# Decoder layer on one core: own order of each engine before the first scores, a transposed maximum, and another bank for eight turns

## The reference, cut to what matters

```python
x = x + attn(layernorm(x), wq, wk, wv, wo)       # 32 query heads, 8 key/value heads, rotary, causal softmax
x = x + einsum("emk,enk->emn",
               quant_1x128(layernorm(x)),        # scale per row and block of 128
               quant_128x128(ctx_2048))          # scale per block of 128 x 128
x = x + moe(layernorm(x), Wg, W1, W3, W2, sw1, sw3, sw2)
# quant_128x128: amax = max |w| over a block of 128 rows and 128 columns, w in fp8 of w * 448 / amax
```

## Time and profile before

| | |
|---|---|
| median of 3 runs | 1612.51 us (1610.12 to 1615.79) |
| the profiled execution's own time | 1612.85 us |
| its span | 1611.0 us |
| PE busy | 1465.1 us (91%) |
| DVE busy | 1213.7 us (75%) |
| POOL busy | 1020.4 us (63%) |
| ACT busy | 948.4 us (59%) |
| chain that ended last | PE 68%, DVE 14%, ACT 7%, issue 5% |

### The profile page before, as it was taken

The page is one execution under the profiler, slowest core; times in us unless marked ns, Lnnn a source line. Parts: engine busy times, 40 slices in busy tenths (PEclk is TensorE's granted clock), DMA queues, the critical chain, the costliest instruction groups (busy, mean ns, idle before and its releaser), DMA issues.

```text
span 1611.0 us, 26917 instructions
## 1 busy us (share of the span) xinstructions
PE 1465.1 (91%) x8616; PEld 1280.9 (80%) x8616; DVE 1213.7 (75%) x2951; ACT 948.4 (59%) x2384; POOL 1020.4 (63%) x1007
## 2 busy tenths in 40 slices
PE   5799999999798999999999998676989899899997
PEld 4588888887677888888888887565788888799996
DVE  6678888887777777878878787986767665587785
ACT  2477787776466678877878878523121213565662
POOL 1687887885776788888888888642303132354555
PEclk9899999999899999999999999897899999899998
DMA  5345444333132334334434433123010002577777
GB/s 188 98 126 165 135 134 134 109 87 100 49 102 50 88 85 118 98 90 115 113 81 109 120 81 89 33 88 91 27 27 27 8 27 84 176 240 221 227 217 239
DMA packets 106588, 177.04 MB, mean 110 GB/s; under 512 B 16662, under 2 KB 38422, under 8 KB 106448
## 3 DMA queue, kind: packets, MB, share of 16 engines
q1 hardware_dynamic: 103888, 167.07, 35.8%
q0 software_dynamic: 2560, 8.25, 1.6%
HBM read 97.28 MB, written 31.98 MB: 80 GB/s over the span
## 4 chain that ended last, share of the span: by engine, by line
PE 68%; DVE 14%; ACT 7%; issue 5%; DMA 2%; POOL 2%; SPq 1%; DVEq 0%; ACTq 0%; POOLq 0%
PE bank L417 15%; PE bank L419 14%; PE bank L418 14%; PE bank L459 6%; PE bank L435 4%; PE bank L474 4%; PE bank L475 4%; PE bank L436 4%; ACT P L762 3%; PE bank L409 2%; DVE P L1038 2%; DVE Opair L1073 1%; ACT xnx L784 1%; DVE work L987 1%; ACT Otmp L768 1%
## 5 line engine op out<-in xcount | busy, mean ns | idle before, releaser
L762 ACT ACTIVATE P<-P,mn 128x512 f32<-128x512 f32 (+3 forms) x512 | 285.0, 557 | 222.5 <-DVE mn L1038 218.9
L1444 POOL TENSOR_TENSOR P<-P,ri 128x128 f32<-128x128 f32 (+3 forms) x512 | 360.2, 735 | 30.2 <-DVE ri L1027 30.2
L1038 DVE CUSTOM_DVE_ANT_0 P<-bank,mask 128x512 f32<-128x512 f32 (+3 forms) x512 | 236.7, 481 | 117.6 <-PE bank L436 116.0
L1079 DVE TENSOR_TENSOR PTl<-bank,PTh 128x512 fp32r<-128x512 f32 (+1 forms) x384 | 229.6, 599 | 33.4 <-ACT PTh L774 30.8
L459 PE MATMUL bank<-ident,P 128*128 128x128 f32 x1280 | 204.7, 275 | 6.9 <-POOL P L1444 6.9
L435 PE MATMUL bank<-KT,QT 128*128 128x256 f32 (+2 forms) x512 | 190.7, 373 | 17.5 <-DVE mn L1038 17.3
L774 ACT ACTIVATE PTh<-bank 128x512 fp32r<-128x512 f32 (+1 forms) x384 | 197.4, 515 | 12.9 <-PE bank L459 10.0
L417 PE MATMUL bank<-XT,Wh 128*128 128x512 f32 x384 | 166.0, 432 | 11.1 <-DVE qcs L1051 6.2
L474 PE MATMUL bank<-PTh,VS 128*128 128x256 f32 (+2 forms) x512 | 163.6, 330 | 13.0 <-DVE PTl L1079 8.7
L436 PE MATMUL bank<-KT,QT 128*128 128x256 f32 (+2 forms) x512 | 167.7, 328 | 0.0
L459 PEld LDWEIGHTS bank<-ident,P 128*128 128x128 f32 x1280 | 151.8, 141 | 7.7 <-POOL P L1444 7.6
(11 more groups left out here) (194 smaller groups left out, 4237.8 us busy)
## 6 DMA issues: line engine op xcount, KB each, us to landing
RW<-in_wf SPq DMA_DIRECT2D x170, 256.0 KB, 3.1
QT<-qh SPq DMA_DIRECT2D x256, 64.0 KB, 2.0
QT<-ql SPq DMA_DIRECT2D x256, 64.0 KB, 2.0
Oraw<-in_wo SPq DMA_DIRECT2D x16, 512.0 KB, 5.3
KT<-KT SPq DMA_DIRECT2D x32, 256.0 KB, 3.0
xnx<-in_ctx SPq DMA_DIRECT2D x32, 256.0 KB, 3.4
Wraw<-in_wqkv SPq DMA_DIRECT2D x9, 768.0 KB, 5.3
saved<-Wh SPq DMA_DIRECT2D x7, 768.0 KB, 3.5
```

Source lines behind the costliest of these rows:

```text
L762: e.activation(pq, pq, ACT.Exp, bias=mn[:, z, qb:qb + 1], scale=-1.0, accum_out=rs[:, z, qb:qb + 1]).then_inc(a_exp, 1)
L1038: e.tensor_tensor_reduce(P[:, z, off[qb]:off[qb] + k], bank[n % 2][:, 0:k], mask[:, 512 - k:512], -0.125, BIG, ALU.add, ALU.min, mn[:, z, ...
L1079: e.tensor_tensor(pt_part(PTl, part), bank[2 + part][:, 0:128 * n].rearrange("p (m n) -> p m n", n=128), pt_part(PTh, part).bitcast(F32), ...
L1444: e.tensor_tensor(pq, pq, ri[:, z, qb:qb + 1].to_broadcast([128, n]), ALU.mult).then_inc(g_norm, 1)
```

## The change

Four things are changed; the arithmetic of the output stays.

1. The loop starts at h = 0. What was in h = -8 to -1 is written out ahead of it for each engine in an order of its own. ACT splits all three parts of the first weights ahead of its first copies. PE projects unit 0 in one piece, turns tiles 4 to 7 in banks 0 to 3, turns the values, and projects unit 1 in one piece. DVE takes the four rotations of unit 0 between the statistics of batch 1 and their inverse deviations. POOL makes `ql` of unit 0 ahead of the key's rotation; before it came behind. SP issues the keys' and queries' DMAs of unit 0 in one row.
2. DVE's statistics of batches 2 and 3 move into h = 0 to 3, two tiles in each, and their inverse deviations to h = 5.
3. Tiles 8 to 15 are turned in bank 2 in place of bank 5. `first_turn` waits for the readers of `turn_p(h - 2, 0)`, and the next `turn_p(..., 0)` waits for the readers of the turned tile.
4. The maximum over partitions is taken by a transpose on PE at h = 46 (128 x 64 into a free part of bank 4), a DVE reduction of 64 x 128, a DMA of the 64 numbers to DRAM at h = 48 and one that spreads them over 128 partitions at h = 49. `turn_p(45, 2)` waits for the reduction. `context_scales` moves from h = 49 to h = 51. POOL's call goes.

The core of the diff:

```diff
+AT_PEAK = 46
@@ wait_bank5
-            elif user == "first_turn":
-                need.wait_ge(v_x, h - 6)
-            elif h == 3:
-                wait_xt(need, 6)
             elif h < 8 or h - 8 >= NH - 11:
...
-            elif 52 <= h - 1 < 60:
-                wait_xt(need, h - 44)
@@ PE: turn_v
-                else:
-                    wait_xt(need, 5)
+                need.wait_ge(v_vl, u)
@@ PE
+            def turn_maxima():
+                need.wait_ge(v_cmax, NCTX)
+                need.wait_ge(a_pt, 3 * (AT_PEAK - 2))
+                need.wait_ge(v_pt, 3 * (AT_PEAK - 2))
+                e.transpose(bank[4][0:64, 256:384], wam[:, :, :].rearrange("p i c -> p (i c)"), ident[:, :]).then_inc(p_cmax, 1)
@@ PE: turn_p
+                if part == 0 and 51 <= h < 59:
+                    wait_xt(need, h - 42)
+                if part == 2 and h == AT_PEAK - 1:
+                    need.wait_ge(v_peak, 1)
@@ PE: ahead of the loop
-            for h in range(-8, NH + 7):
+            for part in range(3):
+                for c in range(4):
+                    project(0, part, c)
+            for t in range(TB, 2 * TB):
+                wait_xt(need, t - TB + 1)
+                first_turn(t, t - TB)
+            turn_v(0)
+            for part in range(3):
+                for c in range(4):
+                    project(1, part, c)
+            for h in range(NH + 7):
@@ PE: in the loop
+                if h == AT_PEAK:
+                    turn_maxima()
...
                 if 52 <= h < 60:
-                    wait_bank5(need, h, "first_turn")
-                    first_turn(h - 44, 5)
+                    need.wait_ge(a_pt, 3 * (h - 2) + 1)
+                    need.wait_ge(v_pt, 3 * (h - 2) + 1)
+                    first_turn(h - 44, 2)
@@ ACT: ahead of the loop
+            for part in range(3):
+                split_wq(0, part)
             for t in range(TB):
                 first_turn(t, t)
-                if t < 3:
-                    split_wq(0, t)
+            values_keys(0)
+            for t in range(TB, 2 * TB):
+                first_turn(t, t - TB)
+            query_hi(0)
+            value_hi(0)
+            key_hi(0)
+            split_wq(1, 0)
+            split_wq(1, 1)
@@ DVE
+            def context_peak():
+                need.wait_ge(p_cmax, 1)
+                e.tensor_reduce(wsc[0:64, 1, 0:1], bank[4][0:64, 256:384], AX.X, ALU.max).then_inc(v_peak, 1)
             def context_scales():
-                need.wait_ge(g_call, 1)
+                need.wait_ge(d_peak[1], 16)
@@ DVE: ahead of the loop, behind first_stats of tiles 4 to 7
+            for fn in range(2):
+                rotate(0, 0, fn)
+            for fn in range(2):
+                rotate(0, 1, fn)
             rstd_of(slice(TB, 2 * TB))
             for t in range(TB, 2 * TB):
                 first_norm(t)
+            key_cos(0)
+            for t in range(TB, 2 * TB):
+                first_turn(t, t - TB)
+            value_lo(0)
+            for fn in range(2):
+                rotate(1, 0, fn)
+            for fn in range(2):
+                rotate(1, 1, fn)
@@ DVE: in the loop
-                if h == 49:
+                if h == AT_PEAK + 5:
                     context_scales()
...
+                if h == AT_PEAK:
+                    context_peak()
...
-                elif h < 0:
-                    first_stats(2 * h + 16)
-                    first_stats(2 * h + 17)
-                if h == -1:
+                if h < 4:
+                    first_stats(2 * h + 8)
+                    first_stats(2 * h + 9)
+                if h == 5:
                     rstd_of(slice(2 * TB, 4 * TB))
@@ POOL: ahead of the loop
+            rotate(0)
+            query_lo(0)
+            rotate_key(0)
+            key_lo(0)
+            split_wq_lo(1, 0)
+            rotate(1)
@@ POOL: in the loop
-                if h == 45:
-                    need.wait_ge(v_cmax, NCTX)
-                    e.partition_all_reduce(wsc[:, 0, :], wam[:, :, :].rearrange("p i c -> p (i c)"), 128,
-                                           bass.bass_isa.ReduceOp.max).then_inc(g_call, 1)
@@ SP: ahead of the loop, behind load_wo(0)
+            load_wq(1)
+            turn_keys(0)
+            place_queries(0, 0)
+            place_queries(0, 1)
+            double_keys(0)
@@ SP: in the loop
+                if h == AT_PEAK + 2:
+                    need.wait_ge(v_peak, 1)
+                    e.dma_start(peak.unsqueeze(1), wsc[0:64, 1, 0:1]).then_inc(d_peak[0], 16)
+                if h == AT_PEAK + 3:
+                    need.wait_ge(d_peak[0], 16)
+                    e.dma_start(wsc[:, 0, :], peak.partition_broadcast(128)).then_inc(d_peak[1], 16)
```

More of the change, by code:

```diff
@@ L182, in decoder @@
         saved = nc.dram_tensor("saved", (NSAVE, 2, 128, 4, 384), F32).ap()
+        peak = nc.dram_tensor("peak", (4 * NCTX,), F32).ap()
         oe = nc.dram_tensor("oe", (NE * CAP, D), F32).ap()
@@ L214, in decoder @@
         v_bm, v_bq, g_badd, g_bq = sem("v_bm"), sem("v_bq"), sem("g_badd"), sem("g_bq")
+        p_cmax, v_peak, d_peak = sem("p_cmax"), sem("v_peak"), [sem("d_peak_out"), sem("d_peak_in")]
         v_cmax, v_cscale, v_q, v_turn, v_x2, v_xn3, v_lt, v_cum, v_place, v_idx, v_piece, v_hm, v_h, v_x3, v_out = (
@@ L217, in decoder @@
                                     "hm", "h", "x3", "out"))
-        g_own, g_pad, g_wq, g_wo, g_norm, g_rot, g_ql, g_ks, g_k, g_kl, g_o, g_zero, g_call, g_t2, g_q, g_const, g_piece = (
-            sem(f"g_{n}") for n in ("own", "pad", "wq", "wo", "norm", "rot", "ql", "ks", "k", "kl", "o", "zero", "call", "t2", "q",
+        g_own, g_pad, g_wq, g_wo, g_norm, g_rot, g_ql, g_ks, g_k, g_kl, g_o, g_zero, g_t2, g_q, g_const, g_piece = (
+            sem(f"g_{n}") for n in ("own", "pad", "wq", "wo", "norm", "rot", "ql", "ks", "k", "kl", "o", "zero", "t2", "q",
                                     "const", "piece"))
@@ L680, in tensor_engine @@
                     attn_out(h - 7)
-                if h < -4:
-                    t = h + 12
-                    if t >= 6:
-                        wait_xt(need, t - 5)
-                    first_turn(t, (4, 5, 0, 1)[t - TB])
                 if 52 <= h < 60:
-                    wait_bank5(need, h, "first_turn")
-                    first_turn(h - 44, 5)
+                    need.wait_ge(a_pt, 3 * (h - 2) + 1)
+                    need.wait_ge(v_pt, 3 * (h - 2) + 1)
+                    first_turn(h - 44, 2)
             for s in (-8, -7, -6):
```

## The result

The changed kernel takes 1589.41 us, the median of four executions (1583.48 to 1593.72); the kernel before, beside it, 1612.30. The ratio is 0.9854, 95% interval 0.9817 to 0.989: faster by 1.5%, 22.9 us, where 32.8 were forecast (1580.0). It lies in the predicted range. The profiled execution took 1588.92 us for a span of 1587.1.

The account below looks back on a forecast made before the run. PE was taken to bound the plain head loop, with something else last in three stretches; 16.3 (maximum) + 8.5 (turns) + 8.0 (start) = 32.8 us off 1612.85 gave 1580.0 us, range 1570 to 1593.

Parts of the forecast that it names:

- The maximum: Heads 46 to 49: dropping POOL's call removes its 13.0 us and the backlog, scales cost 2.0; 16.3 us off.
- The turns: Eight iterations from 452 to 528 us: bank 2 removes PE's 10.5 us of waits for DVE's X; 8.5 us off.
- The start: Way to the first scores and first heads: earlier scores, less the cost of statistics and inverse deviations; 8.0 us off.
- the first scores start at 43.4: Start, on PE: DVE's new order and SP's issues bring the first scores 9.8 us earlier than 53.16.
- Normalising at 25.1: Start, on DVE: four rotations go ahead of the inverse deviations, so normalising starts near 25.1 instead of 22.30.
- takes them at 44.1: 14.6 us earlier: Start, on DVE: it takes the first scores at 44.1 instead of 58.73, no longer busy with inverse deviations.
- Statistics and inverse deviations: DVE, h = 0 to 3 and h = 5: of 6.8 and 5.1 us, 4.2 and 2.5 are paid.
- DVE gives the start back: Rival: statistics, inverse deviations and scales at full price, turns save only 4 us; 1592 us, chance 8%.
- Slower: DVE locked out: Rival: six moved small DVE instructions each lose 6.2 us to rows of POOL work; 1617 us, chance 2%.
- The new way costs what the old one did: Rival: SP or the scales wait for the maximum's two chained DMAs, so part 4 gives nothing; 1596 us, chance 4%.
- turns save nothing: Rival: with turns in bank 2, the wait for the copy moves to `turn_p`; 1588.5 us, chance 5%.
- The rule against one price: Line 1017's 6.46 us: DVE waits for POOL's next gap; by the one-instruction rule 5 us could stay, giving 1585 us.

Follow-up runs that it names:

- the turns alone: The changed kernel with tiles 8 to 15 turned in bank 5 again: 1593.64 us in one execution; heads 51 to 59 take 74.45 us, in the changed kernel 65.80.
- the experiment: The changed kernel with the maximum over partitions put back as one POOL call (h = 45, scales at h = 49): 1602.06 us, ratio 0.9934.
- the 26 trains: Three kernels with a prologue ahead of the changed kernel: POOL runs rows of instructions, DVE issues disputed ones into them; the wide subtraction took 0.70 to 1.74 us.

## Why the prediction was right and wrong

- **What bounds the kernel, the side and the range:** right.
- **The maximum, 16.3 forecast:** 16.1 measured at head 51, with the clock noted above in it. The call's 13.0 us on POOL and line 1017's wait went whole, and returned whole when the call did. The scales cost 2.3 us by their records (426.99 to 429.27); 2.0 were taken. The added transpose, reduction and DMAs were covered, as costed.
- **The rule that speaks against this part:** POOL's call costs it 5.77 us and 7.02 us of idle time around 0.54 in the experiment, against 0.27 us of DVE and one transpose. The Trainium skill, page "GPSIMD Engine Reference", section "Engine selection", gives reductions along partitions to GpSimd; for a maximum over 128 partitions in the middle of a full loop the two kernels say the opposite.
- **The turns, 8.5 forecast:** 10.2 measured, 8.7 by the turns alone; the other 1.5 are luck with the clock. PE's 10.5 us went. The copy of the tile held PE once, 2.0 us, where I took 1.8 for two ends. The slow clock that I counted into what stays did not stay: it is 1.00 in the stretch even with the waits back, and 0.97 once with the changed kernel's own code, so it is not theirs. The "7.3 us of work per iteration" of DVE is a slip: it is 7.3 of every 10 us, and 55.44 / 8 = 6.9 per iteration. DVE was further from being last than I said.
- **The start, 8.0 forecast, nothing measured: the failed step.** It is "the first scores start at 43.4"; they started at 50.41. Normalising at 25.1 was 30.92, 5.8 late. Of these, DVE's chain began 3.9 late (26.75 for 22.9, that is 25.1 less eleven times 0.2). 2.5 of the 3.9 are two waits of 1.00 and 1.51 us for PE's projection, which itself began 1.7 later (18.08; 16.35 in the kernel before) and with slow matmuls. The rest was DVE's own: POOL's early subtractions had held it up by 2 us in the first chain, a step I took over from the kernel before although the change moves ACT's splits. The other 2.0 of the 5.8 are two locked instructions of the second chain. I costed the rotations at their 0.6 us each and nothing for who sends whom: the rotation releases POOL, and POOL's rotation falls on the very chain behind it. The turns at a granted clock of 0.72 added 0.7 (high part 35.50; 29.0 forecast). SP's 5.51 and 5.02 us and the keys' 3.1 were as costed.
- **DVE "takes them at 44.1: 14.6 us earlier".** 51.64, 7.1 earlier. A second error hid in this: the first mask is not the ledger's start. In the kernel before DVE came late, when PE had the first scores ready, and needed 3.8 us from mask to head 0. Now it comes behind PE and needs 6.5. So 2.7 us of the lead at the mask were never there.
- **Statistics and inverse deviations, 4.2 + 2.5:** heads 0 to 8 took 59.3 us instead of 54.5: 4.8. Oversized by 1.9.
- **The rivals.** "DVE gives the start back" came nearest in its time (1592), but for another reason. The statistics were not what ate it. "Slower: DVE locked out" named the mechanism, and it had a large part in the start, at 1.0 us per instruction and not 6.2. "The new way costs what the old one did" and "turns save nothing" fell, each by its own experiment.
- **The rule against one price.** In each of the 26 trains DVE's wait ended with the running POOL instruction. The Trainium skill, page "SBUF — State Buffer", section "Who interferes with whom", gives a lock for one instruction, and these agree. The estimate 1585 that hung on it asked whether the 5 us would stay. They did not, since they belonged to the call's backlog. The kernels' waits of 3.04 to 6.46 us go beyond one instruction, against the rule; but three of them end without a gap of POOL's, against my reading. Neither covers both.

## What to carry to other kernels

Before moving work earlier, write down what each moved instruction releases on the other engines, and check that this does not land on the mover's own next chain: here four rotations moved ahead set POOL on eleven small instructions right behind them. Size a lead at the first event that both kernels reach under the same limit (here the reciprocal of head 8), not where one engine happened to be late before. Cost a call on POOL by the idle time around its record, and by the backlog that follows. Where a single execution is compared, first find the event up to which the two kernels are the same: a lead that is there already is luck.

## What the runs showed of the hardware that was not expected

- DVE's small instructions of the inverse deviations, with 4 to 8 columns, take 0.16 us alone and often 0.9 to 1.2 with POOL at work, 2.26 once. The reciprocal of 4 columns does not: 0.17 at 412.62 in the kernel before, inside a row of POOL's. Statistics and reductions over 512 columns from SBUF take 0.67 in both cases. The longest of the trains' reductions beside POOL's row, nine in a row, took 5.43, 0.60 each.
- In the trains, POOL lost some 0.45 us to each wide subtraction of DVE (2.93 for 2.48), so the lock costs both.
- The partition maximum's second idle time, 6.71 us before and 7.02 in the experiment, comes behind the call, with work waiting.
- The same start, in kernels that differ only after it, put head 8 at 117.43, 116.20 and 115.53 us. The stretch of the turns took 65.8 us at a granted clock of 1.00 and 67.4 at 0.97, with the same code.
